# Moving the bias adds behind the residual adds, and the head sum into TensorE, in a four-lane transformer block

## The reference

```python
x = x + layernorm(L0_attn(layernorm(x)))
x = x + layernorm(L0_ffn(layernorm(x)))
# L1 attention, for each of 4 layers i, on z = layernorm(x):
lo = local_attn(q[:, :4], k[:, :4], v[:, :4])
go = causal_linear_attn(q[:, 4:], k[:, 4:], v[:, 4:])
z = z + concat(lo, go) @ Wo[i] + bo[i]
z = z + gelu(layer_norm(z) @ W1[i] + b1[i]) @ W2[i] + b2[i]
# layer_norm(z) = (z - mean) * rsqrt(var + 1e-5) * g + b
x = x + layernorm(z)
```

## Time and profile before

| | |
|---|---|
| median of three runs | 3571.32 us |
| the profiled execution | 3575.66 us, its span 3573.3 us |
| mean granted TensorE clock | 0.891 of full speed |
| busy shares of the span | PE 81%, DVE 63%, ACT 51%, POOL 13% |
| DMA over the span | 14 GB/s |

### The profile page before, as it was taken

How to read it: one execution, slowest core, us unless ns; L and a number is a source line. 1 busy time by engine, 2 the same in 40 slices (tenths; PEclk the granted TensorE clock), 3 DMA queues, 4 the chain that set the end, 5 groups by cost and what they waited for, 6 DMA issues and landing times.

```text
span 3573.3 us, 75807 instructions
## 1 busy us (share of the span) xinstructions
PE 2902.2 (81%) x31896; PEld 2310.0 (65%) x31896; DVE 2267.0 (63%) x5990; ACT 1824.1 (51%) x4086; POOL 473.3 (13%) x543
## 2 busy tenths in 40 slices
PE   5788888788888848878887688997888899787895
PEld 3566665456666647777777476885767688575574
DVE  4665555665655568988897756347566634764437
ACT  3546555555665457777776354334444433444232
POOL 1110000210000032222221102110010201002000
PEclk8889988888999968998999699997989999798897
DMA  2000000000000010000000100001010000101000
GB/s 92 1 1 1 1 1 1 1 1 1 1 1 2 1 54 7 7 7 7 7 4 1 60 3 24 1 13 37 3 48 3 25 1 2 48 3 48 0 1 25
DMA packets 16996, 48.95 MB, mean 14 GB/s; under 512 B 1168, under 2 KB 9616, under 8 KB 14096
## 3 DMA queue, kind: packets, MB, share of 16 engines
q1 hardware_dynamic: 16656, 44.10, 3.6%
HBM read 41.99 MB, written 2.10 MB: 12 GB/s over the span
## 4 chain that ended last, share of the span: by engine, by line
PE 53%; DVE 32%; ACT 11%; issue 3%; POOL 1%; DMA 0%; SPq 0%; DVEq 0%; POOLq 0%; ACTq 0%
PE ps L324 7%; DVE LN L2012 5%; PE ps L315 5%; PE ps L1890 3%; PE ps L1352 3%; PE ps L381 3%; PE ps L468 3%; DVE M L484 2%; PE ps L289 2%; DVE RS L239 2%; DVE LN L2025 2%; PE ps L1363 2%; ACT LN L263 2%; PE ps L1834 2%; PE ps L789 2%
## 5 line engine op out<-in xcount | busy, mean ns | idle before, releaser
L297 ACT COPY LN<-ps 128x512 f32<-128x512 f32 (+6 forms) x560 | 286.1, 545 | 441.4 <-PE ps L789 108.3
L276 POOL TENSOR_TENSOR RS<-RS,MISC 128x4 f32<-128x4 f32 x184 | 187.3, 1018 | 1565.9 <-DVE RS L258 851.9
L484 DVE TENSOR_REDUCE M<-ps 128x6 f32<-128x768 f32 x256 | 241.3, 954 | 132.7 <-PE ps L468 94.2
L289 PE MATMUL ps<-cons,LN 128*128 128x128 f32 x672 | 128.3, 329 | 184.5 <-ACT LN L263 99.1
L2012 DVE TENSOR_TENSOR LN<-LN 128x1024 f32<-128x1024 f32 (+2 forms) x192 | 219.9, 1145 | 29.1 <-ACT LN L297 17.5
L289 PEld LDWEIGHTS ps<-cons,LN 128*128 128x128 f32 x672 | 91.5, 167 | 227.1 <-ACT LN L263 91.1
L381 PE MATMUL ps<-LN 32*128 32x256 f32 x1024 | 187.7, 441 | 54.3 <-DVE LN L520 31.7
L1890 PE MATMUL ps<-LN,wAB 128*128 128x128 f32 x1024 | 151.7, 311 | 74.8 <-ACT LN L297 74.3
L315 PE MATMUL ps<-LN,wAB 128*128 128x512 f32 x384 | 196.4, 642 | 18.1 <-ACT LN L334 9.4
L384 PE MATMUL ps<-LN 32*128 32x256 f32 x1024 | 202.9, 474 | 4.8 <-DVE M L484 4.3
L1936 ACT ACTIVATE LN<-LN,RS 128x128 f32<-128x128 f32 x512 | 198.6, 400 | 1.6 <-DVE RS L2037 0.6
(11 more groups left out here) (362 smaller groups left out, 7394.2 us busy)
## 6 DMA issues: line engine op xcount, KB each, us to landing
LN<-frame SPq DMA_DIRECT2D x16, 1024.0 KB, 5.1
wAB<-wb SPq DMA_DIRECT2D x16, 256.0 KB, 2.6
LN<-frame SPq DMA_DIRECT2D x8, 512.0 KB, 3.6
LN<-wd SPq DMA_DIRECT2D x8, 512.0 KB, 6.9
wAB<-wa SPq DMA_DIRECT2D x1, 3840.0 KB, 17.4
wCs<-wc SPq DMA_DIRECT2D x1, 2336.0 KB, 10.6
XA<-xin SPq DMA_DIRECT2D x8, 256.0 KB, 8.4
y<-XA SPq DMA_DIRECT2D x8, 256.0 KB, 2.3
```

The lines of the kernel that those rows point to most:

```text
L276: pool.e.tensor_tensor(c.r[:, 40:44], c.r[:, 36:40], mhalf, ALU.pow).then_inc(*c.G.inc((k, "rstd")))
L289: ins = pe.e.transpose(ps[:, n * 128:(n + 1) * 128], src[:, n, :], ident)
L297: act.e.copy(dst, ps).then_inc(*c.A.inc(named(k, done)))
L484: return dve.e.tensor_reduce(cols[:, 2 - 2 * h:4 - 2 * h, :, q.at], src, X_AX, ALU.max, negate=True)
```

## The change

Five things change in phase 1, all of them in `l1` but for the fourth. No result of the layer changes but for rounding.

1. The add of `bo` (L923, round 3) goes to round 12, behind the add of Wo's output, and there waits for it.
2. The add of `b2` (L958, round 15) goes to round 0, behind the add of the perceptron's output, and there waits for it.
3. The DVE add of XT and LT (L941, round 11) goes away. ACT copies the transposed local output into XT instead, and PE multiplies both XT and LT by Wo into the same PSUM columns: eight matmuls in place of four.
4. Minus the mean is no longer computed on DVE (L258). POOL multiplies rstd by the mean and then the product by -1: two operations in place of one. This holds for all 96 norms.
5. `dve_norm` and `dve_stats` get arguments `rms` and `eps`, which no call uses.

```diff
-            dve.e.tensor_scalar(r[:, 36:40], mv[:, :, 1], 1e-5, None, ALU.add).then_inc(*c.D.inc((k, "var")))
+            if rms:
...
+            else:
+                ins = dve.e.tensor_scalar(r[:, 36:40], mv[:, :, 1], eps, None, ALU.add)
+            ins.then_inc(*c.D.inc((k, "var")))
...
-        def dve_stats(dve, c, k, src):
-            next(dve_norm(dve, c, k, src, src))
-            mean = c.r[:, 24:32].rearrange("p (i c) -> p i c", c=2)[:, :, 0]
-            dve.e.tensor_scalar(c.r[:, 48:52], mean, -1.0, None, ALU.mult).then_inc(*c.D.inc((k, "-mean")))
+        def dve_stats(dve, c, k, src, rms=False, eps=1e-5):
+            next(dve_norm(dve, c, k, src, src, rms, eps))
...
         def pool_norm_shift(pool, c, k):
+            mean = c.r[:, 24:32].rearrange("p (i c) -> p i c", c=2)[:, :, 0]
             yield from pool_norm(pool, c, k, False)
-            pool.wait_ge(c.D, (k, "-mean"))
             pool.wait_ge(c.G, (k, "rstd"))
-            pool.e.tensor_tensor(c.r[:, 44:48], c.r[:, 40:44], c.r[:, 48:52], ALU.mult).then_inc(*c.G.inc((k, "shift")))
+            pool.e.tensor_tensor(c.r[:, 44:48], c.r[:, 40:44], mean, ALU.mult).then_inc(*c.G.inc())
+            pool.wait_ge(c.G)
+            pool.e.tensor_tensor(c.r[:, 44:48], c.r[:, 44:48], mone, ALU.mult).then_inc(*c.G.inc((k, "shift")))
             yield
...
-            pe_tr4(pe, c, k, ON1, 1, c.D, "onT")
+            pe_tr4(pe, c, k, ON1, 1, c.A, "onT")
             yield
             ps = c.bank(pe, 0, c.D, (k, "z"))
-            pe.wait_ge(c.D, (k, "onT"))
+            pe.wait_ge(c.A, (k, "lin"))
+            pe.wait_ge(c.A, (k, "onT"))
             for t in range(4):
                 s = slice(t * 128, (t + 1) * 128)
-                ins = pe.e.matmul(ps[:, s], XT[:, s], wv(f"l1o{i}"), start=True, stop=True)
+                pe.e.matmul(ps[:, s], XT[:, s], wv(f"l1o{i}"), start=True, stop=False)
+                ins = pe.e.matmul(ps[:, s], LT[:, s], wv(f"l1o{i}"), start=False, stop=True)
...
-            dve.wait_ge(c.A, (k, "normed", 3))
-            dve.e.tensor_tensor(Z, Z, rep4(wv("bo")[:, i * 128:(i + 1) * 128]), ALU.add).then_inc(*c.D.inc((k, "bo")))
...
-            dve.wait_ge(c.A, (k, "lin"))
-            dve.wait_ge(c.P, (k, "onT_tr"))
-            dve.e.tensor_tensor(XT, c.ps[1][:, :], v["LT"].rearrange("p b c -> p (b c)"), ALU.add).then_inc(
-                *c.D.inc((k, "onT")))
...
-            dve.wait_ge(c.D, (k, "bo"))
             dve.e.tensor_tensor(Z, Z, v4(c.ps[0]), ALU.add).then_inc(*c.D.inc((k, "z")))
+            dve.wait_ge(c.D)
+            dve.e.tensor_tensor(Z, Z, rep4(wv("bo")[:, i * 128:(i + 1) * 128]), ALU.add).then_inc(*c.D.inc())
...
-            dve.wait_ge(c.A, ((g, i, "ln2"), "normed", 3))
-            dve.e.tensor_tensor(Z, Z, rep4(wv("b2")[:, i * 128:(i + 1) * 128]), ALU.add).then_inc(*c.D.inc((k, "b2")))
...
-            dve.wait_ge(c.D, (k, "b2"))
             dve.e.tensor_tensor(Z, Z, v4(c.ps[0]), ALU.add).then_inc(*c.D.inc((k, "y")))
+            dve.wait_ge(c.D)
+            dve.e.tensor_tensor(Z, Z, rep4(wv("b2")[:, i * 128:(i + 1) * 128]), ALU.add).then_inc(*c.D.inc())
...
+            act_copy(act, c, k, v["XT"], c.ps[1][:, :], "onT_tr", "onT")
```

More of the change, by code:

```diff
@@ L231, in ended, with dve_norm @@
                 s.mark(key)
-        def dve_norm(dve, c, k, src, dst):
+        def dve_norm(dve, c, k, src, dst, rms=False, eps=1e-5):
             r = c.r
@@ L245, in dve_norm @@
             dve.wait_ge(c.D)
-            dve.e.tensor_scalar(r[:, 36:40], mv[:, :, 1], 1e-5, None, ALU.add).then_inc(*c.D.inc((k, "var")))
+            if rms:
+                dve.e.tensor_tensor(r[:, 32:36], mv[:, :, 0], mv[:, :, 0], ALU.mult).then_inc(*c.D.inc())
+                dve.wait_ge(c.D)
+                ins = dve.e.scalar_tensor_tensor(r[:, 36:40], r[:, 32:36], eps, mv[:, :, 1], ALU.add, ALU.add)
+            else:
+                ins = dve.e.tensor_scalar(r[:, 36:40], mv[:, :, 1], eps, None, ALU.add)
+            ins.then_inc(*c.D.inc((k, "var")))
             yield
@@ L250, in dve_norm @@
                 rs = r[:, 40 + i:41 + i]
-                ins = dve.e.tensor_scalar(dst[:, i, :], src[:, i, :], r[:, 24 + 2 * i:25 + 2 * i], rs,
-                                          ALU.subtract, ALU.mult)
+                if rms:
+                    ins = dve.e.tensor_scalar(dst[:, i, :], src[:, i, :], rs, None, ALU.mult)
+                else:
+                    ins = dve.e.tensor_scalar(dst[:, i, :], src[:, i, :], r[:, 24 + 2 * i:25 + 2 * i], rs,
+                                              ALU.subtract, ALU.mult)
                 ins.then_inc(*c.D.inc((k, "normed", i)))
-        def dve_stats(dve, c, k, src):
-            next(dve_norm(dve, c, k, src, src))
-            mean = c.r[:, 24:32].rearrange("p (i c) -> p i c", c=2)[:, :, 0]
-            dve.e.tensor_scalar(c.r[:, 48:52], mean, -1.0, None, ALU.mult).then_inc(*c.D.inc((k, "-mean")))
+        def dve_stats(dve, c, k, src, rms=False, eps=1e-5):
+            next(dve_norm(dve, c, k, src, src, rms, eps))
         def act_norm(act, c, k, src, dst):
@@ L732, in pe_l1 @@
             CP = v["CP"].rearrange("p (b u c) -> p b u c", b=2, c=128)
+            LT = v["LT"].rearrange("p b c -> p (b c)")
             k = (("l1", g // 4, i), c.n)
@@ L955, in dve_l1 @@
             yield
-            k = (g, i, "mlp")
-            dve.wait_ge(c.A, ((g, i, "ln2"), "normed", 3))
-            dve.e.tensor_tensor(Z, Z, rep4(wv("b2")[:, i * 128:(i + 1) * 128]), ALU.add).then_inc(*c.D.inc((k, "b2")))
             yield
             yield
+            k = (g, i, "mlp")
             dve.wait_ge(c.P, (k, "sum"))
-            dve.wait_ge(c.D, (k, "b2"))
             dve.e.tensor_tensor(Z, Z, v4(c.ps[0]), ALU.add).then_inc(*c.D.inc((k, "y")))
+            dve.wait_ge(c.D)
+            dve.e.tensor_tensor(Z, Z, rep4(wv("b2")[:, i * 128:(i + 1) * 128]), ALU.add).then_inc(*c.D.inc())
             if i == 3:
```

## The result

The changed kernel takes 3617.06 us, the median of four runs from 3605.19 to 3625.88, against 3572.39 us before (the median of four here): ratio 1.0119, 95% interval 1.0098 to 1.0140. It is 44.7 us slower. The profiled execution took 3610.3 us. The chance of 0.89 for slower and the predicted 3615 us held.

What follows compares the result with a forecast made beforehand. Phase 1 was taken as bound by a ping-pong chain of waits between engines, not by one engine. Terms of 17.2 + 3.6 + 17.0 + 5.8 + 3.4 - 1.8 - 1.0 = 44.2 us on 3571.32 gave 3615, range 3588 to 3642.

Steps and rivals of the forecast that it cites:

- Only the place on the chain counts: Throughout phase 1, an operation costs time only where the chain of waits goes through it; no size of its own.
- The biases, 20.8 us net of L258: Bias adds behind L963 and L947: 26 places at 0.66 us, 17.2 us, plus 3.6 us for L647.
- the second kind: Rounds with only the bo add behind Wo's residual add on DVE: 0.66 us later each, net of L258.
- a rival, with one more stretch in each of 17 rounds and 20 us: PE's clock in phase 1 falls more often as DVE is late longer: 20 us for eight times 17 rounds, 3635; chance 0.17.
- the main case: Whole kernel: the sum of the terms as worked out, 3601 to 3630 us, chance 0.60.
- The passes, 0.945 each: Wo's matmuls on PE: eight more passes cost 0.945 us in each of 18 chain places, 17.0 us.
- in the remaining 14 layers PE is not late: Wo's round in the other 14 layers: DVE's sum ends later, so the added passes cost nothing there.
- the estimate made by it: Wo's added passes at about 81 ns per matmul: 0.65 us for eight, 11.7 us instead of 17.0.
- the chain never goes the way by L941: Ahead of Wo's matmuls: removing DVE's L941 shortens the way by 0.69 us, but off the chain, so no gain.
- L647, 0.6 us in six rounds: DVE's task behind L963: moves by about 0.6 us in a round recurring six times, 3.6 us.
- ACT's copy, 5.8 us: The copy into XT on ACT: 0.58 us in six places and 0.39 in six, 5.8 us.
- The norms, 3.4 us for POOL: POOL's second operation in the norms: 0.34 us more in ten chain places, 3.4 us.

Runs made afterwards that it cites:

- e11_nobias: The kernel before with both bias adds and the waits for them taken out, so its output lacks them: ratio 1.0009.
- e1_bias: The kernel before with only the two bias adds moved behind the residual adds: 3606.52 us against 3569.21, ratio 1.0101.
- e7_copy: The kernel before with ACT's copy into XT and without DVE's add; only XT multiplied by Wo, LT left out: ratio 0.9998.
- e2_sum: The kernel before with only the head sum changed: ACT copies, PE multiplies XT and LT, DVE's add gone: 3595.24 us, ratio 1.0074.
- e4_passes: The kernel before with DVE copying into XT instead of adding, and PE multiplying XT and LT by Wo: 3594.21 us, ratio 1.0078.
- e8_triple: The kernel before with the four matmuls by Wo issued three times each, 16 more passes per layer: 3621.29 us, ratio 1.0145.
- e3_pool: The kernel before with only minus the mean times rstd moved to two POOL operations, DVE's L258 gone: 3576.94 us, ratio 1.0021.

## Why the prediction was right, and where its terms were not

The total, 44.2 us predicted and 44.7 measured, is partly good luck: the chain took more places than were counted, each with less of its price, and the clock added an estimated 4 to 6 us. Point by point:

**Only the place on the chain counts: right.** e11_nobias shows that the bias adds cost nothing where they stood, e1_bias that they cost where they went: 16 us at equal clock, 37 with the clock. Taking 32 adds from DVE in e7_copy brought nothing that the whole kernel shows.

**The biases, 20.8 us net of L258: nearly right by place, but with the clock at nothing.** They measured 37 us alone (e1_bias), of which 16 are left at equal clock. In the round of both adds the delay is as predicted, 1.40 for 1.32, and ahead of L647 too (below). Behind the second kind it is 0.35 for 0.66. The step that failed is the one that let these delays pass on to the end unchanged: PE's half-clock stretches move, give back 1.27 us at one place and take 1.6 at another. I had this as a rival, with one more stretch in each of 17 rounds and 20 us. For the biases alone it holds in full, beside the main case and not in place of it. In the changed kernel the clock loss grew by 8.6 and 16.8 us in two profiles, and the clock of its executions is lower by 0.0019 and 0.0026, an estimated 4 to 6 us: about a quarter of the rival's size.

**The passes, 0.945 each: right in size, wrong in number.** 0.91 more in the chain at 1034 us. But "in the remaining 14 layers PE is not late" failed. With the passes added the chain goes by the products 30 times (e2_sum), 29 (e4_passes) and 31 (e8_triple) for 18; at equal clock the three cost 30, 25 and 57 us where the sums had 23, 17 and 34 to 45. In the changed kernel it is 22 times, since there the moved adds are on the chain in some of these places, 15 and 15 times where I had 16 and 10. In a row of the new products each pass takes 0.22 / 2 = 0.11 us. The Trainium skill (TensorE: Matmul & The Clock Gate, section Back-to-back issue gap) has about 81 ns for a matmul of 128 columns in a sustained stream; the trace of these fp32 passes doesn't agree, and the estimate made by it was too low.

**DVE's relief: one thing overlooked.** I wrote that the chain never goes the way by L941. L941 isn't on it at the third place either, the gap from the fourth lane to the first, but it stands in DVE's queue ahead of what PE waits for there. Chain rows of L801 at that place, first of the kernel before, then of e7_copy (L802, without L941), then of the changed kernel, where the matmuls go from 1085.77 to 1087.55:

```profile
1063.81 1.16 PE ps L801 x8
```

```profile
1059.91 0.89 PE ps L802 x8
```

```profile
1085.77 0.22 PE ps L812 x2
```

Eight passes took 1.16 us before and take 0.89 without L941, the latter as in the last row. The weight loads (PEld) of the two kernels, before and e7_copy, show the holder, L917 (L918 in e7_copy), the last DVE reader of the PSUM bank that L801 fills:

```profile
1063.81 0.86 PEld L801 LDWEIGHTS ps<-wAB,LN 128*128 128x128 f32 x7 [0.84 <-DVE LN L917]
```

```profile
1059.41 0.19 PEld L802 LDWEIGHTS ps<-wAB,LN 128*128 128x128 f32 x1 [0.33 <-DVE LN L918]
1059.75 0.86 PEld L802 LDWEIGHTS ps<-wAB,LN 128*128 128x128 f32 x7 [0.15 <-issue]
```

Before, L917 ends at 1063.76 and the first load starts at 1063.81, when L315, the matmuls ahead, has ended too. In e7_copy L918 ends at 1059.36, the first load is over at 1059.60, while L315 still runs to 1059.91, and the products follow without a stop. e11_nobias has the gap at the same 19.08 us, with L941 still there and L958 gone: either add out of DVE's queue ahead brings L917 forward. So the passes cost 1.78 - 1.16 = 0.62 there, not 0.945. A number in a row that was larger than its sisters (1.16 for 0.91) was there to be read.

**L647, 0.6 us in six rounds: right in the round looked at.** The chain of the changed kernel, DVE without a gap from L960 to L656 (before: L953 and L647):

```profile
1077.42 0.71 DVE LN L960
1078.13 0.18 DVE MISC L656
```

From the residual add at 1074.62 this is 3.51 us; before it was 1056.07 - 1053.15 = 2.92: 0.59.

**ACT's copy, 5.8 us: too high.** It adds 0.40 where I had 0.58, and 0.07 where I had 0.39. A copy's row is longer than the distance at which copies follow each other, the same trap as L258's 0.16 us for 0.07, which I had avoided on DVE. e7_copy shows no cost, as the 0.27 us of relief make up for it.

**The norms, 3.4 us for POOL:** its part is 0.22 us each, so some 2 us in ten places. The 7.7 us of e3_pool are more than this, and they come with 6.5 us of clock loss in its profile; at equal clock 1 us is left.

The parts alone add up to 37 + 26 + 8 = 71 us, the whole change has 45 to 48. Most of this is the clock: at equal clock the parts are 16 + 30 + 1 = 47, the whole 39 to 42. The rest, 5 to 8 us, fits the chain: in the whole it passes the products 22 times for 30 and the adds 30 times for 32, as one covers the other. How many us each such place gives back wasn't measured. What this teaches of my sum: the terms of place at equal clock are smaller than I had (about 5.2 us in 17 rounds: 0.07, then 1.40 + 0.40 + 0.91 + 0.35, then 0.91, then 0.59 + 0.62, which is 5.25, where the sum had 0.39, 3.50, 0.95 and 1.55, which is 6.39), eight times 5.25 make 42 us, and the clock moves this by several us either way from one execution to the next. That eight times 5.25 come out so near is luck in part: the terms are read in one round of each kind, and leave out the 1.27 us that PE gave back there.

## What to carry to other kernels

An operation costs what it costs in its place: read for each moved instruction whether the chain passes where it was and where it goes, and price it by the distance from start to start in a row of its kind. Work that stands in an engine's idle time is already free; moving it behind the value that everybody waits for makes it dear, even when the engine's busy time falls. Count the places anew when work is added to the engine that is late next, since the chain moves there: 18 places became 30 here. And where TensorE stops and starts, compare two stretches or two sets of executions only at the same granted clock, and take several profiles before an effect of one per cent is put down to one instruction.

## What was not expected of the hardware

The lost clock comes in steps. In all these kernels the loss of a gap in the steady rounds is near 0, 1.8, 3.5, 5.1, 6.9 or 8.6 us, and one step makes the gap from the first lane to the second 1.6 us longer. A change of well under one microsecond in DVE's work, or the removal of work, moves a kernel from one pattern to another: e11_nobias does less than the kernel before, and its twelve executions have a clock of 0.8901, the kernel before 0.892 to 0.893 over 57. Of all that were run without more work on PE the kernel before has the highest; with more work (e2_sum, e8_triple) it is 0.895. The Trainium skill (TensorE: Matmul & The Clock Gate, section What's actually happening) says that the clock follows how busy the array has been; the fall ahead of 998 us comes behind a wait of PE for DVE, and the one near 1007 us behind a stretch, 1002 to 1007, in which PE was busy for 3.41 of 5 us, which agrees. A stretch at half clock can also be cheap: from 1007 us on PE was busy at half speed (4.52 of 5 us), but the chain went by DVE and nobody waited for PE; the work that PE started at 1015 us then ran at full speed. The gap as a whole lost the same as the one before, 5.1 us.
